# Attention units in pairs: scores of both, then 128-row products of both, then values of both

## The reference

```python
q, k, v = (xn @ W for W in (Wq, Wk, Wv))            # 16 heads of 64
probs   = softmax(q @ k.T / 8)                        # per batch and head, 512 x 512
att     = (probs @ v) @ Wo
a       = layer_norm(xn + att, gamma, beta)
# mixture of experts: top 2 of 8, renormalised
g, u    = xn @ gate_w[e] + gate_b[e], xn @ up_w[e] + up_b[e]
f       = sum over e of p[e] * ((silu(g) * u) @ down_w[e] + down_b[e])
out     = x + a + f
```

## Time and profile before

| | |
|---|---|
| time, median of 3 runs | 499.82 us (499.13 to 500.76) |
| profiled execution, first to last instruction | 486.1 us |
| granted TensorE clock | 0.998 of full speed |
| busy TensorE / VectorE / GpSimd / ScalarE | 97% / 83% / 79% / 64% |

### The profile page before, as it was taken

The page is one execution under the profiler, slowest core; times in us unless marked ns, Lnnn a source line. Parts: engine busy times, 40 slices in busy tenths (PEclk is TensorE's granted clock), DMA queues, the critical chain, the costliest instruction groups (busy, mean ns, idle before and its releaser), DMA issues.

```text
span 486.1 us, 8501 instructions
## 1 busy us (share of the span) xinstructions
PE 473.7 (97%) x3003; PEld 309.4 (64%) x3003; DVE 404.1 (83%) x657; ACT 310.7 (64%) x482; POOL 383.5 (79%) x331
## 2 busy tenths in 40 slices
PE   8999999999999999999999999999999999999994
PEld 5766555666665666666556666666666589998642
DVE  5878888888888998889998888888888976666766
ACT  4776667666777666666666676666666745554641
POOL 5998787777899786899988888878888956666874
PEclk9999999999999999999999999999999999999999
DMA  8940111211100003000000000000000223321422
GB/s 263 236 70 3 44 45 38 49 25 31 34 1 1 5 1 86 2 1 1 1 16 15 14 14 17 16 12 18 17 12 16 63 62 86 82 80 42 120 59 87
DMA packets 27662, 21.74 MB, mean 45 GB/s; under 512 B 3089, under 2 KB 25175, under 8 KB 27620
## 3 DMA queue, kind: packets, MB, share of 16 engines
q1 hardware_dynamic: 25348, 16.95, 13.7%
q0 software_dynamic: 2272, 4.24, 2.7%
HBM read 13.19 MB, written 8.40 MB: 44 GB/s over the span
## 4 chain that ended last, share of the span: by engine, by line
PE 71%; POOL 16%; DVE 4%; ACT 4%; issue 4%; POOLq 0%; DVEq 0%; ACTq 0%
PE psum L425 14%; PE psum L440 13%; PE psum L412 5%; PE psum L431 4%; POOL psums L1249 4%; POOL psums L1245 4%; PE psum L465 4%; PE psum L618 4%; POOL psums L1234 3%; PE psum L400 3%; PE psum L402 2%; PE psum L401 2%; PE psum L595 2%; PE psum L456 2%; PE psum L597 2%
## 5 line engine op out<-in xcount | busy, mean ns | idle before, releaser
L763 ACT ACTIVATE probs<-psum 128x1024 f32<-128x1024 f32 x128 | 131.2, 1027 | 65.9 <-PE psum L431 59.7
L936 DVE TENSOR_REDUCE q_top<-psum 128x2 f32<-128x1024 f32 x128 | 150.9, 1221 | 8.1 <-PE psum L412 7.3
L440 PE MATMUL psum<-probs,v_now 128*64 128x512 f32 x512 | 115.9, 594 | 0.0
L1234 POOL TENSOR_TENSOR psums<-probs 128x1024 f32<-128x1024 f32 x32 | 76.7, 2395 | 32.2 <-ACT probs L763 31.4
L1249 POOL TENSOR_TENSOR psums<-psums 128x512 f32<-128x512 f32 x64 | 81.8, 1299 | 2.5
L1245 POOL TENSOR_TENSOR psums<-probs 128x1024 f32<-128x1024 f32 x32 | 76.2, 2380 | 1.4 <-ACT probs L763 1.3
L440 PEld LDWEIGHTS psum<-probs,v_now 128*64 128x64 f32 x512 | 35.3, 137 | 60.4 <-issue 56.5
L425 PE MATMUL psum<-q_hi,k_hi 64*128 64x512 f32 x256 | 56.0, 432 | 0.5 <-ACT probs L763 0.5
L412 PE MATMUL psum<-k_hi,q_hi 64*128 64x512 f32 x256 | 51.8, 399 | 1.3 <-DVE o_norm L969 0.9
L425 PE MATMUL psum<-q_lo,k_hi 64*128 64x512 f32 x256 | 50.9, 392 | 0.0
L425 PE MATMUL psum<-q_hi,k_lo 64*128 64x512 f32 x256 | 50.8, 391 | 0.0
(11 more groups left out here) (226 smaller groups left out, 939.3 us busy)
## 6 DMA issues: line engine op xcount, KB each, us to landing
xs_sorted<-sums SPq DMA_DIRECT2D x10, 260.0 KB, 7.6
xs_in<-xs_sorted SPq DMA_DIRECT2D x10, 260.0 KB, 2.9
y_in<-ys SPq DMA_DIRECT2D x8, 256.0 KB, 4.4
rest<-in_L_attn_h_dram SPq DMA_DIRECT2D x4, 256.0 KB, 5.4
stage<-in_L_ffn_gate_w_dram SPq DMA_DIRECT2D x8, 128.0 KB, 2.1
acc<-in_L_ffn_gate_w_dram SPq DMA_DIRECT2D x8, 128.0 KB, 3.0
stage<-in_L_ffn_up_w_dram SPq DMA_DIRECT2D x8, 128.0 KB, 2.9
acc<-in_L_ffn_up_w_dram SPq DMA_DIRECT2D x8, 128.0 KB, 3.4
```

The lines of the kernel that those rows point to most:

```text
L440: mm = pe.matmul(o[DH * h:DH * h + DH, :], v_now[:, kt, at:at + DH], probs[:, par, kt, h, :], start=(kt == 0), stop=(kt == TB - 1))
L763: act.activation(probs[:, u % 2, kt, :, :], psum[:, bank:bank + 2, :], ACT.Exp, scale=SCALE)\
L936: dve.tensor_reduce(tops[:, :, qt], psum[:, mx_bank(qt):mx_bank(qt) + 2, :], AX.X, ALU.max)\
L1234: pool.tensor_tensor(psums[:, par, :, :], probs[:, par, 0, :, :], probs[:, par, 1, :, :], ALU.add)\
```

## The change

The 32 units become 16 pairs, numbered g, with units a = 2g and b = 2g + 1. TensorE does all scores of a and b (with the rough scores of the next pair in between), then all 128-row products for both, then denominators and values of both, of the same pair and no longer of the unit before. What follows from it, in other places:

- high and low parts of keys and queries are kept for four units (`kq_hi`, `kq_lo`) and are copied for key and query together, 128x1024; the shifts of two units are set together; buffers are laid out anew to make room (x is loaded a second time, later, and so are the experts' second weights);
- the shares of both units are added in one bank (`output_share(pair)`), so `add_share` runs once a pair;
- a first pair with an order of its own (`first_pair`), in which TensorE projects for units 2 to 5 and takes rough scores up to unit 3;
- the sums of unit 31's exponents are made by VectorE (`sums_of_last`), not GpSimd; only units 0 to 3 are in `WHOLE`;
- the experts come before pair 15 (`END`), and small jobs move to other places in their engines' lists.

```diff
-        WHOLE = (0, 1, 2, 3, HOST - 1, LAST)
+        WHOLE = (0, 1, 2, 3)
...
+            def output_share(pair):
...
+                pe.wait_ge(added, pair)
+                pe.wait_ge(o_ready, 2 * pair + 2)
                 for t in range(TB):
+                    for u in (2 * pair, 2 * pair + 1):
+                        mm = pe.matmul(psum[:, share_bank, P * t:P * t + P], o_parts[u % 2][:, P * t:P * t + P],
+                                       wo_sb[:, u % NP, :], start=(u % 2 == 0), stop=(u % 2 == 1))
                 mm.then_inc(wo_ready, 1)
...
+            def first_pair():
...
+                pe.wait_ge(lo_ready, 8)
+                project(5)
+
+                pe.wait_ge(v_kept, slices_before(1))
+                denominators(0)
+                values(0, 0)
+                values(0, 1)
+                pe.wait_ge(lo_ready, 10)
+                scores_for_max(3, 0)
+                pe.wait_ge(lo_ready, 12)
+                scores_for_max(3, 1)
+                values(0, 2)
+                values(0, 3)
+                scores_for_max(3, 2)
+                scores_for_max(3, 3)
+                pe.wait_ge(shift_ready, 3)
+                for kt in range(TB):
+                    values(1, kt)
+                denominators(1)
+                turn_max_by_head(3)
+
+            def pair_scores(g):
+
+                a = 2 * g
+                for u in (a, a + 1):
+                    for kt in range(TB):
+                        if u == a and kt == 0:
+                            pe.wait_ge(shift_ready, a + 2 if g > 1 else a + 1)
+                            if g < END:
+                                pe.wait_ge(lo_ready, 4 * g + 8)
...
+                        if u == a and kt == 1:
+                            pe.wait_ge(inv_ready, 4 * g - 1)
+                        if u > a or kt >= 2:
+                            pe.wait_ge(probs_ready, 4 * u + kt - 1)
+                        scores(u, kt)
+                        scores_shift(u, kt)
+                        if g < END:
...
+                            if u == a and kt == 1:
+                                pe.wait_ge(o_ready, a)
+                                if g >= 2:
+                                    pe.wait_ge(added, g - 1)
+                            scores_for_max(u + 2, kt)
+
+            def pair_products(g):
+
+                a, b = 2 * g, 2 * g + 1
+                pe.wait_ge(probs_ready, 4 * b + 3)
+                if g < END - 1:
+                    project(a + 4)
+                    pe.wait_ge(top_ready, 4 * b + 8 + 3)
+                    project(b + 4)
+                pe.wait_ge(probs_ready, 4 * b + 4)
+                for t, half, bank in slices(g):
                     project_v(t, half, bank)
+                if g < END:
+                    if g < END - 1:
+                        pe.wait_ge(lo_ready, 2 * a + 10)
+                    turn_max(a + 2)
+                    turn_max(b + 2)
+                output_share(g - 1)
+                if 2 <= g <= 4:
+                    route_logits(g - 1, 6, 0)
+                if g <= 3:
+                    turn(g)
+                if g == 7:
                     count_slots()
+                if g == 9:
                     sum_table()
+                if g == END - 1:
+                    turn_group(0)
+
+            def pair_values(g):
+
+                a, b = 2 * g, 2 * g + 1
...
+                denominators(a)
+                for kt in range(TB):
+                    values(a, kt)
...
+                values(b, 0)
+                denominators(b)
+                for kt in range(1, TB):
+                    values(b, kt)
...
+            def pair(g):
+                a, b = 2 * g, 2 * g + 1
+                exponents(a)
+                exponents(b)
+                if a not in WHOLE:
+                    round_sums(a, 0)
+                if g < END - 1:
+                    upper(a + 4)
+                if a not in WHOLE:
+                    round_sums(a, 1)
+                if g < END - 1:
+                    upper(b + 4)
+                for n in range(slices_before(g), slices_before(g + 1)):
+                    keep_slice(n)
...
+                if g <= 3:
+                    copy_xt(g)
+                if 2 <= g <= 5:
+                    round_w(2 * g - 4)
+                    round_w(2 * g - 3)
+                guess_inverse(a)
+                if b not in WHOLE:
+                    round_sums(b, 0)
+                    round_sums(b, 1)
+                if g <= 2:
+                    norm(g + 1)
+                if g == 1:
+                    inverse_root(3)
+                if g == END - 1:
+                    round_group(0)
+                guess_inverse(b)
...
+            def sums_of_last():
+                dve.wait_ge(probs_ready, 4 * LAST + 2)
+                total, part = psums[:, LAST % 2, :, :], (probs[:, LAST % 2, kt, :, :] for kt in range(TB))
+                dve.wait_ge(den_ready, LAST - 1)
+                dve.tensor_tensor(total, next(part), next(part), ALU.add).then_inc(last_sums, 1)
+                for n in range(2):
+                    dve.wait_ge(probs_ready, 4 * LAST + 3 + n)
+                    dve.wait_ge(last_sums, n + 1)
+                    dve.tensor_tensor(total, total, next(part), ALU.add).then_inc(last_sums, 1)
...
+                lower(5)
+                variances(2)
+                maximum(3, 0)
+                maximum(3, 1)
+                invert(0)
+                invert_more(0)
+                normalise(0)
+                maximum(3, 2)
+                maximum(3, 3)
+                set_shift(3)
+                invert(1)
+                invert_more(1)
+
+            def pair(g):
+                a, b = 2 * g, 2 * g + 1
+                normalise(a - 1)
+                if g == END:
                     experts()
+                    sum_y(B - 1)
+                    sums_of_last()
+                    sum_y(B - 2)
+                if g < END:
+                    for u in (a + 2, b + 2):
+                        for qt in range(TB):
+                            maximum(u, qt)
+                if a not in WHOLE:
+                    lower_sums(a, 0)
+                if g < END - 1:
+                    lower(a + 4)
+                if a not in WHOLE:
+                    lower_sums(a, 1)
+                if g < END - 1:
+                    lower(b + 4)
+                if g < END:
+                    set_shifts(a + 2)
+                add_share(g - 1)
...
+                if b not in WHOLE:
+                    lower_sums(b, 0)
+                invert(a)
+                if b not in WHOLE:
+                    lower_sums(b, 1)
+                invert_more(a)
...
+                normalise(a)
+                invert(b)
+                invert_more(b)
+                if g == END - 1:
                     lower_group(0)
                     keep_weights(0)
...
+                for u in (2 * g, 2 * g + 1):
+                    if u < LAST:
+                        first_sums(u)
+                        other_sums(u)
+                extra(g)
```

More of the change, by code:

```diff
@@ L436, in values @@
                 pair, par = u % NP, u % 2
[L437 removed]
+                o = psum[:, o_at(u), :]
                 for h in range(2):
@@ L1214, in _ @@
                 maximum(0, t)
-            lower(1, 1)
+            lower_part(1, 1)
             set_shift(0)
-            lower(1, 0)
-            for u in range(UNITS):
-                unit(u)
-            normalise(LAST - 1)
-            sum_y(B - 2)
-            invert(LAST)
-            invert_more(LAST)
+            lower_part(1, 0)
+            first_pair()
+            for g in range(1, PAIRS):
+                pair(g)
             last_norm()
```

707 lines of the change are left out of this document (364 added, 343 removed).

## The result

The changed kernel takes **532.8 us** (median of 4 runs, 528.5 to 536.2) beside 499.5 for the kernel before on the same chip: ratio 1.065, 95% interval 1.0605 to 1.0703. It is slower, as forecast, but by 33 us and not by 6, far outside the range.

What follows compares the result with a forecast made beforehand. TensorE, busy 97% of the span, was taken as the bound. 75.5 + 317.5 + 62.9 + 0.9 + 35.0 = 491.8 us against 486.1; with the median 13.7 above the span, 505.5 us, range 499.5 to 511.

Steps and rivals of the forecast that it cites:

- the price of `lower_sums`: VectorE in pairs 2 to 14: four `lower_sums` of 0.73 us within 21 of 23.9 us a pair.
- Modes, and the steps of scores: TensorE, pairs 2 to 14: fewer tiling mode changes gain 8.1 us; eight score steps in a row lose 0.9.
- rival 1: Pairs run shorter than 23.9 us because mode changes cost more; decides from 23.35 a pair, 494 us at 23.0; chance 0.10.
- merged copies: ScalarE and VectorE, pairs 2 to 14: some 1 to 2 us a pair freed, covered by TensorE, so no gain.
- even on the edge: Second unit's denominators: chain of 4.65 us against TensorE's 4.74; 0.1 a pair over ten pairs, 1.0 us lost.
- pairs 2 and 3: ScalarE's `copy_xt` and two `round_w` precede the first unit's `guess_inverse`, chain ends 1.2 late: 2.4 us lost (0 to 4).
- Pair 14: Projects nothing, so `turn_max` waits for the eighth maximum and second denominators for sums: 2.5 us lost (1 to 3.5).
- The first pairs: Start of the kernel: 7.7 us more work done and 3.1 lost in waits, so pair 2 starts at 75.5.
- The tail: From unit 30's first scores: TensorE stands 5.3 us until `lower_sums(30)`, behind VectorE's y and last sums; 35.0 us in all.
- Rival 3: The clock falls in the tail's stand; work behind it runs at 1.2 GHz, 2 us more: 507.5 us; chance 0.30.
- Rival 4: VectorE becomes the bound as GpSimd stretches its two-input instructions; second denominators' chain 5.2, 0.5 a pair: 512 us; chance 0.13.
- 13.7 above the profiled span: The median of the runs, 499.8 us, against the profiled span of 486.1; the difference was added unchanged to the forecast.

Runs made afterwards that it cites:

- e11_whole: The changed kernel with fp32 sums straight into TensorE for all units, so no `round_sums` or `lower_sums`: 509.4 us, ratio 1.025 to the kernel before.
- e6_gap: The changed kernel, GpSimd starting a pair's second sums only after the first unit's `lower_sums`, with ScalarE's rounding and VectorE's `lower_sums` moved ahead: 524.8 us, ratio 1.053.
- e13_before_whole: The kernel before with fp32 denominators in all units, no `round_sums` and no `lower_sums`: 509.4 us, ratio 1.017 to the kernel before.
- e1_order: The changed kernel with VectorE making both residues, `lower(a+4)` and `lower(b+4)`, before the two `lower_sums` of unit a: 541.1 us, ratio 1.082.
- e3_tail: The changed kernel with VectorE making, in the last pair, unit 30's `lower_sums` first, then `sums_of_last`, then the y sums: 528.6 us, ratio 1.056.

## Why the prediction was wrong

**Where the 33 us are**, in ratios. Splitting the sums (`round_sums` on ScalarE and `lower_sums` on VectorE, which leave the kernel together in e11_whole) costs the merged kernel 1.065 - 1.025 = 0.040, 20 us, more than float32 denominators do. In the kernel before the same split saves 0.017, 9 us. Merging without it costs 1.025 - 1.017 = 0.008, 4 us. The three make 33.

**The step that failed** is the price of `lower_sums`: "4 x 0.73" in VectorE's sum for a pair, and 0.7 in the chain to the second denominators. It was taken from rows of a kernel in which GpSimd pauses where `lower_sums` runs. The idle time was in the view (21.9 us in 17 units before L1234), and the prediction even used that GpSimd starts 3.65 after the pair's start; it did not go on to ask what GpSimd does when VectorE gets to `lower_sums(a)`. By its own numbers the first unit's sums end at 3.65 + 7.3 = 10.95, and the second unit's follow at once; measured, that is 10.94 (198.25 - 187.31), and `lower_sums(a, 0)` comes 0.14 later. That e6_gap, with the pause put back, has the line at 0.82 again and products at 6.5, and that e11_whole without the line has pairs of 24.7 to 25.2 and a middle 6.9 shorter than e13_before_whole, shows the cause. The pause alone doesn't win the time back (6 of 33 us), since it delays the second unit's sums.

**Point by point.**
- Modes, and the steps of scores: right. Scores 9.63, values 7.85, and up to 0.56 a pair in e11_whole. (The sum has 6.7 for 13 x 0.51 = 6.6, and the time stays the same at 23.46 a pair, not at rival 1's 23.35; neither matters.)
- The 1 to 2 us a pair that merged copies free on ScalarE and VectorE: VectorE's busy time in pairs 2 to 14 is 318 us, not less than the 286 of the earlier trace rows but more, since a blocked instruction counts as busy.
- Second denominators "even on the edge", and pairs 2 and 3: values of pairs 2 to 5 took 10.1, 9.3, 9.0 and 8.5, a loss of 5.5 against the forecast's 2.4 for two pairs. In e11_whole all are 8.73 or 8.74, what they cost without a wait: the chain's excess was the split of the sums as well.
- Pair 14: lost 3.2 in products and 3.0 in values, against 2.5 for both, and its scores took 10.7 for 9.6, for which the forecast had nothing. In e11_whole its products are 2.9, but its values still 10.3.
- The first pairs: 75.5 forecast, 77.6 measured. In twelve profiles of the merged kernel and its variants pair 2 starts at 75.5 to 75.8 in six and at 77.2 to 77.6 in six; the step was right for half of them.
- The experts' first wait: 1.3 forecast, 1.28 measured.
- The tail: the stand was there, 7.2 for 5.3. The adds beside GpSimd were the term that was too small, 6.6 for 3.9, and `sum_y(3)` with 2.99 for 1.4. The prediction worked out 7 us from what the Trainium skill (SBUF — State Buffer, Who interferes with whom) says. The trace agrees that such instructions are held up; the 7 is partly luck, since three waits of 1.3 in place of the 0.5 already in the sum give 8.7. The same rule, had it been asked of the pairs, was the warning. Rival 3 came true with it: half clock behind the stand, priced 2, measured 2.3. Its comparison of 5.3 with 4.8 us does not carry over: the clock also fell behind waits of 2 us.
- Rival 4 was the right mechanism with the wrong place and a quarter of the size. It looked at unit b's chain and gave 0.5 a pair. The waits were at unit a's `lower_sums`, 1.1 to 1.2 in most pairs and 3.5 with half clock in one.
- "13.7 above the profiled span; I leave that as it is": not around the span, but an untypical execution. Its experts and tail were carried over as they were, so the difference forecast is not touched.

**What stays open**: why the experts take 62 us in one profile and 68 to 73 in all others; other banks and leaving out the moved rows didn't change it; why pair 8's long wait comes in some executions only; what sets whether half clock follows a wait of 2 to 3 us. Also what the scatters do to the scores of the next pair (below).

## What to carry to other kernels

A duration is that of an instruction in its company: before moving an instruction, look up what the engine that shares its ports does at the new time, not only whether its own engine is free. Where two engines contend, a pause in one of them is a resource, and a merge of two loops that closes the pause must pay for it. A busy share counts being kept out as work, so read the mean and the spread of each line as well; and take a second profile before using the distance between span and median.

## What was unexpected of the hardware

- A VectorE instruction that GpSimd keeps out need not be let in between two of GpSimd's adds that follow one another: in pair 8 one took 5.25 us that takes 0.68 alone. In pair 6 it was let in behind the first add (2.86 and 1.73 us).
- Clock: a wait of TensorE of 2 to 3 us is followed by half clock in some places and not in others. In e1_order the grant over the 3.1 us behind a wait of 2.07 was 0.56 in pair 6, and it stayed 1.00 behind the same 2.07 in pair 5. In front of pair 14's first denominators a wait of 3.10 in the changed kernel was followed by 0.57 over 4 us, one of 3.22 in e3_tail by 1.00. Behind the 1.12 of pair 6 no drop showed, behind pair 8's 3.5 it was 0.57. No length of a wait that decides it can be read from these rows.
- Behind GpSimd's scatters VectorE and ScalarE resume together, late. Scores of pair 11, four engines:

```profile
319.47 0.39 PE L470 MATMUL psum<-shift,ones_r 64*128 64x512 f32 x2
319.52 0.96 POOL L1599 DMA_INDIRECT xs_sorted<-xn,pos  x1 [0.30 <-issue]
319.70 0.39 PE L443 MATMUL psum<-kq_hi 64*128 64x512 f32 x2
...
321.74 2.36 DVE L1093 TENSOR_REDUCE q_top<-psum 128x2 fp32r<-128x1024 f32 x2 [1.64 <-PE psum L443]
321.78 1.94 ACT L879 ACTIVATE probs<-psum 128x1024 f32<-128x1024 f32 x2 [4.31 <-PE psum L470]
```

The first exponent usually starts 1.3 us after the first score; here 3.1 after it (318.67), and the first maximum within 0.04 of it, though their matmuls had ended 1.7 to 1.9 us earlier. Without the scatters it doesn't occur in pairs 10 to 13. Through what, no run here shows.
